# Index rows, key-bias rows and softmax sums taken from TensorE to VectorE, and the score weights requested first on SyncE's queue

## The chip, the cores and the metric

One NeuronCore of a Trainium2 chip runs the whole kernel. The metric is device microseconds of one execution. Five engines run their own instruction streams and meet at semaphores: TensorE (PE; its weight loads are shown apart as PEld), VectorE (DVE), ScalarE (ACT), GpSimd (POOL) and SyncE (SP), whose queue issues nearly all DMAs.

## The reference

Per batch of 8, ten rows of `base_hidden` (224 x 512) are chosen by a linear score, attend with 16 heads of 32 columns to 750 rows of `scaffold_hidden`, and the result replaces those ten rows.

```python
scores = jnp.einsum('bnd,d->bn', base_hidden, score_w[0]) + score_b[0]
_, topk_idx = jax.lax.top_k(scores, TOPK)                      # TOPK = 10
sparse_hidden = jnp.take_along_axis(base_hidden, topk_idx[:, :, None], axis=1)
q = (sparse_hidden @ Wq.T + bq).reshape(B, TOPK, H, dh).transpose(0, 2, 1, 3)
k = (scaffold_hidden @ Wk.T + bk) ...                          # same for v, with S = 750
logits = jnp.einsum('bhqd,bhkd->bhqk', q, k) * scale
attn = jax.nn.softmax(logits, axis=-1)
o = jnp.einsum('bhqk,bhkd->bhqd', attn, v).transpose(0, 2, 1, 3).reshape(B, TOPK, D)
attn_out = o @ out_w.T + out_b
return base_hidden.at[jnp.arange(B)[:, None], topk_idx].set(attn_out)
```

## The kernel before

Everything is float32. The key and value projections are folded away: `fold_keys` and `fold_pairs` multiply the queries by Wk, so that the logits of a batch are 24 matmuls of the raw context (`logits_by_step`, line 773, `logits`, line 787: six tiles of 125 context rows by four steps of 128 columns, for 160 query-head columns), and `weigh` (line 806) is 24 matmuls that weigh the raw context with the probabilities; `project_values` (821) and `project_output` (834) follow once, at the end. In the trace each of these float32 matmuls is two records, so a batch's `weigh` is 48.

Batches 0 and 1 go first (group 0). Their ten rows are found by ranking and taken from `x_sb` with one-hot matrices; the other six batches (group 1) go by VectorE's `choose_eight` and `choose_rest`, and GpSimd fetches their rows with an indirect DMA (line 286) that waits for `idx_ready`. The row numbers of all 80 rows stand in `row_idx`, one for each partition. Before the change they get there over TensorE: `move_idx` multiplies the one-hot matrices by `row_name` (677) and `idx_diag` by ones (678), and VectorE casts the PSUM column (456). That piece stands inside `weigh(0)`, ahead of its sixth matmul.

`dot_key_bias` (748) is query times key bias: 32 equal columns `key_rep` as weights, and the spread-out queries `q_diag` (each head's columns zero elsewhere; 40 columns for each batch) as the moving side. ScalarE (343, group 0) or VectorE (488, group 1) copies the result to `key_rows`, and a transposing reduction (493) makes `key_dot` of it.

The softmax's shift comes over VectorE: `find_max` (503) and `find_shift` (509 to 527) and `subtract_max` (535); ScalarE takes the exponential (352), which `weigh` of that batch waits for; `sum_probs` (541) adds over the six tiles. The sum over partitions is `sum_rows` (755), eight records on TensorE inside the last `weigh`, then a reciprocal over 128 x 320 (546). `finish_heads` (552, 555) needs it.

SyncE's queue issues in this order: x(0) to x(2), wq, x(3), wk, x(4), the first part of the context columns of batch 0, x(5), two more parts, x(6), a part of batch 1, x(7), two parts of batch 1, then the context rows `ctx_r` of batches 0 and 1 (200). `score(b)` (404) is VectorE's dot product of x(b) with the score weights, which TensorE spreads over the partitions (631) as soon as `score_line` is in; that 2 KB row was requested by ScalarE's queue (298).

Of the kernel before, what the change touches and what calls it, by code (L numbers as in the profile page):

```python
# [17 lines left out]
ALU = mybir.AluOpType  # L18
# [6 lines left out]
P = 128  # L25
# [28 lines left out]
def build(nc, x, x_lines, ctx_rows, ctx_cols, wq, wk, wv, wo, in_bias, out_b, score_row, out):  # L54
# [5 lines left out]
    with stack:  # L60
# [42 lines left out]
        idx_diag = sb("idx_diag", [GB, BQ])  # L103
# [8 lines left out]
        key_rep = sb("key_rep", [P, DT, QUAD])  # L112
        key_rows = sb("key_rows", [QUAD, B, DT, HC])
        key_dot = sb("key_dot", [QUAD, B, CB])
# [7 lines left out]
        prob_sum = sb("prob_sum", [S_P, B, HQ])  # L122
# [25 lines left out]
        row_idx_ps = misc_ps[1][0:BQ, N:N + 1]  # L148
# [17 lines left out]
        idx_diag_done, idx_moved, idx_ready = sem("idx_diag_done"), sem("idx_moved"), sem("idx_ready")  # L166
# [8 lines left out]
        key_rep_done, key_rows_done = sem("key_rep_done"), sem("key_rows_done")  # L175
        key_dot_ps, key_dot_done = sem("key_dot_ps"), sem("key_dot_done")
        heads_scaled = sem("heads_scaled")
        shifted, exp_done, sum_done, den_done = sem("shifted"), sem("exp_done"), sem("sum_done"), sem("den_done")
        inv_done = sem("inv_done")
# [11 lines left out]
        def _(sp):  # L191
# [16 lines left out]

            load_x(0, 3)
# [3 lines left out]
            load_x(4, 5)  # L213
            load_cols_part(0, 0)
            load_x(5, 6)
# [37 lines left out]
        def _(pool):  # L253
# [15 lines left out]
            pool.memset(idx_diag[:, :], 0.0).then_inc(consts_cleared, 1)  # L269
# [3 lines left out]
            pool.memset(idx_diag[0:1, TOPK:2 * TOPK], float(N)).then_inc(own_done, 1)  # L273
            pool.memset(regroup[:, :, :], 0.0).then_inc(regroup_done, 1)
            pool.memset(head_mask[:, :], 0.0).then_inc(mask_done, 1)
            for i in range(2 * FIRST):
# [8 lines left out]
            pool.wait_ge(idx_ready, 1)  # L285
# [11 lines left out]
        def _(act):  # L297
            act.dma_start(score_line[:, :], score_row).then_inc(score_w_in, 16)
# [41 lines left out]
            def copy_key_rows():  # L340
                act.wait_ge(key_dot_ps, 1)
                for e in range(DT):
                    nc.scalar.activation(
                        key_rows[:, 0:FIRST, e, :],
                        key_ps[0][e * QUAD:(e + 1) * QUAD, 0:HC * FIRST].rearrange("p (b c) -> p b c", b=FIRST),
                        ACT.Copy).then_inc(key_rows_done, 1)

# [18 lines left out]
            copy_key_rows()  # L366
# [25 lines left out]
        def _(dve):  # L392
# [36 lines left out]
            def choose_rest():  # L429
# [8 lines left out]
                    out=idx_diag[0:nb, b0 * TOPK:b1 * TOPK].rearrange("p (b q) -> p b q", q=TOPK),  # L438
# [44 lines left out]
            def copy_key_dot(g):  # L483
                b0, b1 = GROUPS[g]
                if g:
                    dve.wait_ge(key_dot_ps, 2)
                    for e in range(DT):
                        nc.vector.tensor_copy(
                            key_rows[:, b0:b1, e, :],
                            key_ps[g][e * QUAD:(e + 1) * QUAD, 0:HC * (b1 - b0)].rearrange("p (b c) -> p b c", b=b1 - b0))\  # L490
                            .then_inc(key_rows_done, 1)
# [4 lines left out]
                    AX.X, ALU.max, apply_transpose=True).then_inc(key_dot_done, 1)  # L496
# [42 lines left out]
            def sum_probs(b, n):  # L539
                dve.wait_ge(exp_done, 2 * b + 2)  # L540
                nc.vector.tensor_reduce(prob_sum[:, b, :], probs[n][:, :, :].rearrange("p t c -> p c t"), AX.X, ALU.add)\  # L541
                    .then_inc(sum_done, 1)

            def invert():
                dve.wait_ge(den_done, 1)
                nc.vector.reciprocal(inv_sum[:, :, :].rearrange("p e q -> p (e q)"), misc_ps[0][:, 0:DT * BQ]).then_inc(inv_done, 1)  # L546

            def finish_heads():
                dve.wait_ge(inv_done, 1)
# [8 lines left out]
            def finish_output():  # L558
# [29 lines left out]
            nc.vector.tensor_copy(key_rep[:, :, :], bias_sb[:, 1, :].unsqueeze(2).broadcast_to([P, DT, QUAD]))\  # L588
                .then_inc(key_rep_done, 1)
            dve.wait_ge(mask_done, 1 + HPT)  # L590
            spread_queries(0)
            score(4)
            score(5)
            copy_key_dot(0)
# [6 lines left out]
            choose_rest()  # L601
            find_max(1, 1)
            move_idx()
# [6 lines left out]
            copy_key_dot(1)  # L610
# [5 lines left out]
            invert()  # L616
# [5 lines left out]
        def _(pe):  # L622
# [50 lines left out]
            def move_idx():  # L673
                b0, b1 = GROUPS[1]
                pe.wait_ge(idx_diag_done, 1)
                for j in range(2):
                    nc.tensor.matmul(row_idx_ps, one_hot[:, j, :], row_name[:, j:j + 1], start=(j == 0), stop=False)
                nc.tensor.matmul(row_idx_ps, idx_diag[0:b1 - b0, :], ones[0:b1 - b0, 0:1], start=False, stop=True)\
# [237 lines left out]
```

## Time and profile before

| | us |
|---|---|
| runs of the kernel before | 143.16 median of 3 (143.11 to 146.93) |
| the profiled execution | 142.52, of which the span of the core is 140.7 |
| TensorE busy | 134.0 (95% of the span), 1312 matmul records |
| VectorE busy | 80.4 (57%) |
| ScalarE busy | 25.9 (18%) |
| GpSimd busy | 6.1 (4%) |
| DMA traffic | 37.52 MB, mean 267 GB/s over the span, 400 to 440 GB/s in nearly all of the first 31 us |
| granted TensorE clock | 1.00 of full speed in every stretch up to 120 us |

The chain of waits is the work that ended last, followed back: each piece was released by the one before it. A piece has its start and its length. A group's idle time before it says what it waited for.

### The profile page before, as it was taken

Reading aid. Unit: us, or ns where it says so; the run is one execution under the profiler, and the core shown is the slowest. Engines: PE = TensorE matmul, PEld = TensorE weight load, DVE = VectorE, ACT = ScalarE, POOL = GpSimd, SP = SyncE. Lnnn points to the kernel's source line nnn. Section 1 sums busy time; section 2 is a strip of 40 time slices with the busy share of each in tenths; the row PEclk is TensorE's granted clock in tenths of the full one; section 3 lists DMA queues with packets and bytes.
Section 4 is the critical chain, followed back from the end, with each engine's and each line's share of the span. In section 5 each row is a group of like instructions: output and inputs, shape, how many; then the busy total and the mean of one; then the engine's idle time right before and its main releaser. Section 6 shows DMA issues by size and latency. Waiting matters only on the chain.

```text
span 140.7 us, 3072 instructions
## 1 busy us (share of the span) xinstructions
PE 134.0 (95%) x1312; PEld 127.1 (90%) x1312; DVE 80.4 (57%) x212; ACT 25.9 (18%) x57; POOL 6.1 (4%) x31
## 2 busy tenths in 40 slices
PE   4989999999999999999999999999999999999990
PEld 2567999899999989999999999999999999998970
DVE  1788545999951576288870674088128605754350
ACT  4122410030411240003140041005001400411110
POOL 7400000003000000000000000000000000000002
PEclk9999999999999999999999999999999999999997
DMA  4999999999996299899979976995880380000001
GB/s 138 417 417 418 408 413 399 439 423 433 412 359 286 42 383 399 295 397 410 426 288 290 321 318 188 323 319 219 269 298 11 57 356 38 0 0 5 0 5 49
DMA packets 6959, 37.52 MB, mean 267 GB/s; under 512 B 961, under 2 KB 961, under 8 KB 4642
## 3 DMA queue, kind: packets, MB, share of 16 engines
q1 hardware_dynamic: 6528, 37.00, 69.3%
q0 software_dynamic: 128, 0.33, 0.7%
q8 instruction: 10, 0.16, 0.5%
q10 hardware_dynamic: 290, 0.01, 0.2%
q14 instruction: 3, 0.02, 0.0%
HBM read 33.50 MB, written 3.83 MB: 265 GB/s over the span
## 4 chain that ended last, share of the span: by engine, by line
PE 72%; DMA 14%; SPq 7%; issue 2%; DVE 1%; POOLq 1%; POOL 0%; DVEq 0%
PE mix_ps L806 38%; PE logits_ps L787 23%; DMA ctx_r<-ctx_rows_dram 14%; PE logits_ps L773 5%; SPq L197 3%; SPq L204 3%; PE logits_ps L737 2%; PE logits_ps L703 1%; PE mix_ps L737 1%; POOLq L60 1%; DVE o_T L555 1%; PE misc_ps L821 1%; DVE heads L552 1%; PE misc_ps L755 0%; SPq L210 0%
## 5 line engine op out<-in xcount | busy, mean ns | idle before, releaser
L806 PE MATMUL mix_ps<-probs,ctx_r 125*128 125x160 f32 x384 | 54.3, 301 | 0.1
L806 PEld LDWEIGHTS mix_ps<-probs,ctx_r 125*128 125x128 f32 x384 | 52.6, 190 | 0.9 <-issue 0.5
L787 PE MATMUL logits_ps<-qk,ctx_c 128*125 128x160 f32 x240 | 33.4, 299 | 0.0
L787 PEld LDWEIGHTS logits_ps<-qk,ctx_c 128*125 128x125 f32 x240 | 32.9, 188 | 0.0
L503 DVE TENSOR_REDUCE col_max<-logits_ps 125x160 f32<-125x960 f32 x8 | 9.2, 1154 | 25.5 <-PE logits_ps L787 21.2
L773 PE MATMUL logits_ps<-qk,ctx_c 128*125 128x160 f32 x144 | 20.5, 302 | 0.1
L773 PEld LDWEIGHTS logits_ps<-qk,ctx_c 128*125 128x125 f32 x144 | 19.6, 188 | 0.8 <-issue 0.4
L356 ACT ACTIVATE mix<-mix_ps 128x320 f32<-128x320 f32 x16 | 7.0, 439 | 64.4 <-PE mix_ps L806 64.4
L541 DVE TENSOR_REDUCE prob_sum<-probs 125x160 f32<-125x960 f32 x8 | 14.7, 1846 | 4.0 <-ACT probs L352 4.0
L352 ACT ACTIVATE probs<-probs 125x480 f32<-125x480 f32 x16 | 9.3, 603 | 27.9 <-DVE probs L535 27.9
L404 DVE CUSTOM_DVE_ANT_0 product<-x_sb,score_w_sb 112x513 f32<-112x513 f32 x16 | 10.4, 690 | 4.1 <-DMA x_sb<-x_lines_dram 4.1
L535 DVE TENSOR_TENSOR probs<-logits_ps,shift 125x480 f32<-125x480 f32 x16 | 9.8, 653 | 0.3
L625 PE MATMUL logits_ps<-ones 128*128 128x256 f32 (+2 forms) x8 | 4.1, 629 | 1.1 <-DVE ones L568 1.1
L290 POOL MEMSET pool_woken<- 16x1 f32 x1 | 0.1, 88 | 100.3 <-DVE o_T L555 100.3
L525 DVE COPY head_shift<-head_shift 32x5 f32<-32x5 f32 x24 | 3.9, 163 | 0.8
L513 DVE COPY quad_max<-quad_max 32x5 f32<-32x5 f32 x24 | 3.8, 158 | 0.8
L546 DVE RECIPROCAL inv_sum<-misc_ps 128x320 f32<-128x320 f32 x1 | 2.2, 2157 | 3.5 <-PE misc_ps L755 3.5
L703 PEld LDWEIGHTS logits_ps<-picked_T,wq_sb 128*64 128x64 f32 x128 | 3.9, 138 | 0.2 <-issue 0.2
L703 PE MATMUL logits_ps<-picked_T,wq_sb 128*64 128x20 f32 (+1 forms) x128 | 4.1, 218 | 0.0
L464 DVE TENSOR_TENSOR q_sb<-logits_ps,bias_sb 128x40 f32<-128x40 f32 (+1 forms) x4 | 1.0, 242 | 5.0 <-PE logits_ps L703 5.0
L637 PEld LDWEIGHTS mix_ps<-mix,ones 112*112 112x112 f32 x8 | 1.8, 284 | 1.5 <-ACT mix L306 1.5
L625 PEld LDWEIGHTS logits_ps<-ones 128*128 128x128 f32 x8 | 1.7, 258 | 1.4 <-DVE ones L568 1.1
(121 smaller groups left out, 88.7 us busy)
## 6 DMA issues: line engine op xcount, KB each, us to landing
ctx_r<-ctx_rows_dram SPq DMA_DIRECT2D x8, 1536.0 KB, 7.6
ctx_c<-ctx_cols_dram SPq DMA_DIRECT2D x6, 1500.0 KB, 10.1
x_sb<-x_lines_dram SPq DMA_DIRECT2D x8, 520.0 KB, 9.4
out_dram<-x_sb SPq DMA_DIRECT2D x8, 448.0 KB, 12.4
ctx_c<-ctx_cols_dram SPq DMA_DIRECT2D x2, 750.0 KB, 14.5
ctx_c<-ctx_cols_dram SPq DMA_DIRECT2D x4, 375.0 KB, 15.5
wq_sb<-wq_dram SPq DMA_DIRECT2D x1, 1024.0 KB, 7.4
wk_sb<-wk_dram SPq DMA_DIRECT2D x1, 1024.0 KB, 9.9
```

The lines of the kernel that those rows point to most:

```text
L197: sp.dma_start(ctx_c[b][:, fs, :, :], ctx_cols[b, :, fs, :, :]).then_inc(part_cols_in[b][k], 16)
L352: nc.scalar.activation(part, part, ACT.Exp, scale=SCALE).then_inc(exp_done, 1)
L356: nc.scalar.activation(mix[:, 2 * half:2 * half + 2, :, b * TOPK:(b + 1) * TOPK], mix_ps[half][:, 0:2 * HQ].rearrange("p (t h q) -> p t h ...
L404: nc.vector.tensor_tensor_reduce(out=products[j][:, :], in0=x_sb[0:X_P, b, j, 0:D + 1], in1=score_w_sb[:, :], scale=1.0, scalar=0.0, op0=A ...
L503: nc.vector.tensor_reduce(col_max[0:S_P, :], tiles(n).rearrange("p k t c -> p c k t"), AX.XY, ALU.max)\
L535: nc.vector.tensor_tensor(probs[n][:, k * BANK_T:(k + 1) * BANK_T, :], tiles(n)[:, k, :, :], shift[0:S_P, :].unsqueeze(1).broadcast_to([S_ ...
L541: nc.vector.tensor_reduce(prob_sum[:, b, :], probs[n][:, :, :].rearrange("p t c -> p c t"), AX.X, ALU.add)\
L625: nc.tensor.matmul(logits_ps[1][:, 1, 0:n], ones[:, :], ones[:, 0:1].broadcast_to([P, n]), start=True, stop=True)
L703: last = nc.tensor.matmul(query_ps[g][half][j * TILE:(j + 1) * TILE, k * nq:(k + 1) * nq], wq_sb[:, t, c:c + TILE], picked_T[g][:, t, b0 * ...
L773: last = nc.tensor.matmul(logits_ps[n][0:S_P, t // BANK_T, (t % BANK_T) * HQ:(t % BANK_T + 1) * HQ], ctx_c[n][:, f, t, :], qk[:, b, f, :], ...
L787: last = nc.tensor.matmul(logits_ps[n][0:S_P, t // BANK_T, (t % BANK_T) * HQ:(t % BANK_T + 1) * HQ], ctx_c[n][:, f, t, :], qk[:, b, f, :], ...
L806: last = nc.tensor.matmul(mix_ps[half][:, f * HQ:(f + 1) * HQ], ctx_r[n][0:S_P, t, c:c + P], probs[n][:, t, :], start=(t == 0), stop=(t == ...
```

## The change

Five things change. (1) SyncE's queue issues the score row before everything else, instead of ScalarE's. (2) The first part of batch 0's context columns is issued ahead of x(4) and x(5). (3) `move_idx` leaves TensorE: VectorE adds the rows of `idx_diag` in a transposing reduction (three columns of 32), and four new steps (`name_first`) make the first 20 row numbers, between the key-bias rows and `score(5)`. `move_idx` now stands ahead of `find_max(1)`. (4) `dot_key_bias` takes the narrow queries `q_sb` as the moving side and the bias split by head, `key_heads`, as weights; VectorE multiplies the result with slices of `ident` to spread it over the heads (`spread_key_dot`), for both groups, ScalarE no longer copies. (5) `sum_rows` and the large reciprocal are replaced by `invert`, all on VectorE, once for batches 0 to 6 after `sum_probs(6)` and once for batch 7 after `sum_probs(7)`. TensorE no longer waits for `inv_done`; `finish_heads` does.

```diff
+            sp.dma_start(score_line[:, :], score_row).then_inc(score_w_in, 16)
             load_x(0, 3)
             sp.dma_start(wq_sb[:, :, :], wq).then_inc(wq_in, 16)
             load_x(3, 4)
             sp.dma_start(wk_sb[:, :, :], wk).then_inc(wk_in, 16)
-            load_x(4, 5)
             load_cols_part(0, 0)
-            load_x(5, 6)
+            load_x(4, 6)
...
+            def name_first():
+                dve.wait_ge(names_cleared, 1)
+                cols = slice(0, FIRST * TOPK)
+                nc.vector.tensor_scalar(named[0][0:X_P, cols], one_hot[:, 0, cols], row_name[:, 0:1], None, ALU.mult)\
+                    .then_inc(name_step, 1)
...
+                nc.vector.scalar_tensor_tensor(out=named[1][0:X_P, cols], in0=one_hot[:, 1, cols], scalar=row_name[:, 1:2],
+                                               in1=named[0][0:X_P, cols], op0=ALU.mult, op1=ALU.add).then_inc(name_step, 1)
...
+                nc.vector.tensor_reduce(quad_named[:, 0:1], named[1][:, :].unsqueeze(1), AX.X, ALU.add, apply_transpose=True)\
+                    .then_inc(name_step, 1)
...
             def move_idx():
-                dve.wait_ge(idx_moved, 1)
-                nc.vector.tensor_copy(row_idx[:, :], row_idx_ps).then_inc(idx_ready, 1)
+                dve.wait_ge(idx_diag_done, 1)
+                nc.vector.tensor_reduce(idx_cols[:, :], idx_diag[:, :, :], AX.X, ALU.add, apply_transpose=True).then_inc(idx_summed, 1)
+                dve.wait_ge(idx_summed, 1)
+                dve.wait_ge(name_step, 7)
+                nc.vector.tensor_tensor(row_idx[0:QUAD, :], idx_cols[:, 0:1], first_idx[:, :], ALU.add).then_inc(idx_ready, 1)
+                for k in range(1, QUADS - 1):
+                    m = min(QUAD, BQ - k * QUAD)
+                    nc.vector.tensor_copy(row_idx[k * QUAD:k * QUAD + m, :], idx_cols[0:m, k:k + 1]).then_inc(idx_ready, 1)
...
+            def spread_key_dot(g):
...
+                    nc.vector.tensor_tensor(
+                        key_rows[:, b0:b1, e, :].rearrange("p b (h q) -> p b h q", h=HPT),
+                        key_ps[g][lines, 0:nb * TOPK].rearrange("p (b q) -> p b q", b=nb).unsqueeze(2).broadcast_to([QUAD, nb, HPT, TOPK]),
+                        ident[lines, e * QUAD:e * QUAD + HPT].unsqueeze(1).unsqueeze(3).broadcast_to([QUAD, nb, HPT, TOPK]), ALU.mult)\
+                        .then_inc(key_rows_done, 1)
...
+            def invert(part, b0, b1):
+                at = 7 * part
+                bs = slice(b0, b1)
+                dve.wait_ge(key_dot_done, 2)
+                dve.wait_ge(sum_done, b1)
+                nc.vector.tensor_reduce(
+                    quad_sum[:, 0, bs, :].rearrange("p b k -> p (b k)"),
+                    prob_sum[:, bs, :].rearrange("p b c -> p (b c)").rearrange("p (k c) -> p k c", c=QUAD),
+                    AX.X, ALU.add, apply_transpose=True).then_inc(inv_step, 1)
...
+                for q in range(1, QUADS):
+                    nc.vector.tensor_copy(quad_sum[0:QUAD, q, bs, :], quad_sum[q * QUAD:(q + 1) * QUAD, 0, bs, :])\
+                        .then_inc(inv_step, 1)
...
+                nc.vector.tensor_reduce(all_sum[:, bs, :], quad_sum[0:QUAD, :, bs, :].rearrange("p q b k -> p b k q"), AX.X, ALU.add)\
+                    .then_inc(inv_step, 1)
...
+                nc.vector.reciprocal(inv_all[:, bs, :], all_sum[:, bs, :]).then_inc(inv_step, 1)
...
+                nc.vector.transpose(inv_rows[:, bs, :].rearrange("p b c -> p (b c)").rearrange("p (k c) -> p k c", c=QUAD),
+                                    inv_all[:, bs, :].rearrange("p b k -> p (b k)").unsqueeze(2)
+                                    .broadcast_to([QUAD, (b1 - b0) * CB, QUAD])).then_inc(inv_step, 1)
...
+                for h in range(HPT):
+                    nc.vector.tensor_copy(
+                        inv_sum[h * DH:(h + 1) * DH, :, :].rearrange("p e (b q) -> p e b q", b=B)[:, :, bs, :],
+                        inv_rows[:, bs, :].rearrange("p b (e h q) -> p h e b q", e=DT, h=HPT)[:, h]).then_inc(inv_done, 1)
...
-            weigh(0, 0, {5: move_idx})
+            weigh(0, 0, {})
...
-            weigh(B - 1, (B - 1) % 2, {14: sum_rows})
+            weigh(B - 1, (B - 1) % 2, {})
```

GpSimd clears four more tiles at the start (`key_heads`, `named`, a part of `prob_sum`, and a larger `idx_diag`).

On TensorE's queue, from the end of `logits` of batch 1 into `weigh(0)` and `weigh(1)`, there stands before:

```order
L773 MATMUL logits_ps<-qk,ctx_c 125x160 x16
L806 MATMUL mix_ps<-probs,ctx_r 128x160 x5
L677 MATMUL misc_ps<-row_name,one_hot 80x1 x2
L678 MATMUL misc_ps<-ones,idx_diag 80x1
L806 MATMUL mix_ps<-probs,ctx_r 128x160 x33
L685 MATMUL logits_ps<-ident,picked 128x80 x4
```

and of the changed kernel:

```order
L812 MATMUL logits_ps<-qk,ctx_c 125x160 x16
L845 MATMUL mix_ps<-probs,ctx_r 128x160 x38
L734 MATMUL logits_ps<-ident,picked 128x80 x4
```

The three matmuls inside `weigh(0)` are gone, and nothing stands between `logits` of batch 1 and the transposes of the fetched rows but 38 matmuls of `weigh`.

On VectorE's queue, from the index arithmetic of `choose_rest` to the first step of `find_shift(1)`, there stands before:

```order
L437 SCALAR_TENSOR_TENSOR idx_diag<-top_idx,row_base,own_batch 6x60
L503 TENSOR_REDUCE col_max<-logits_ps 125x160
L456 CAST row_idx<-misc_ps 80x1
L509 TENSOR_REDUCE quad_max<-col_max 128x5
L513 COPY quad_max<-quad_max 32x5 x3
```

and of the changed kernel:

```order
L440 SCALAR_TENSOR_TENSOR idx_diag<-top_idx,row_base,own_batch 6x60
L476 TENSOR_REDUCE idx_cols<-idx_diag 32x3
L479 TENSOR_TENSOR row_idx<-idx_cols,first_idx 32x1
L482 CAST row_idx<-idx_cols 32x1
L482 CAST row_idx<-idx_cols 16x1
L532 TENSOR_REDUCE col_max<-logits_ps 125x160
L538 TENSOR_REDUCE quad_max<-col_max 128x5
```

Four small instructions have come ahead of `find_max(1)`, and the one cast behind it is gone.

On the same queue, from the end of `score(4)` to `find_max(0)` (the rows named ISA are `score`), there stands in the changed kernel:

```order
L516 TENSOR_TENSOR key_rows<-logits_ps,ident 32x2x40 x4
L522 TENSOR_REDUCE key_dot<-key_rows 32x10
L460 TENSOR_SCALAR named<-one_hot,row_name 112x20
L463 SCALAR_TENSOR_TENSOR named<-one_hot,row_name,named 112x20
L466 TENSOR_REDUCE quad_named<-named 128x1
L470 COPY quad_named<-quad_named 32x1 x3
L472 TENSOR_REDUCE first_idx<-quad_named 32x1
L407 ISA product,scores<-x_sb,score_w_sb 112x513
L407 ISA scores 112x1
```

Before, `score(5)` followed `score(4)` at once, and of these rows there was only the reduction to `key_dot`, behind `score(5)`; eleven instructions more now stand ahead of `score(5)`.

## Rows read from the trace of the kernel before

**Rows 1.** The page: shares of the chain of waits by engine.

```profile
PE 72%; DMA 14%; SPq 7%; issue 2%; DVE 1%; POOLq 1%; POOL 0%; DVEq 0%
```

**Rows 2.** Waits: engine and line, what for, us in total, times, longest.

```profile
PEld mix_ps L806 <- DMA ctx_r<-ctx_rows_dram: 0.3, 1, 0.3
```

**Rows 3.** The chain of waits in order of time: start, length, what.

```profile
0.82 0.38 SPq L204
...
11.56 19.48 DMA ctx_r<-ctx_rows_dram
...
31.08 1.63 PE mix_ps L806 x10
32.70 0.22 PE misc_ps L677 x4
...
33.15 9.16 PE mix_ps L806 x66
...
51.55 0.54 PE misc_ps L748 x8
...
58.80 6.52 PE logits_ps L787 x48
```

**Rows 4.** Timeline, 32 to 38 us: start, length, engine, line, what.

```profile
32.04 0.27 DVE L437 SCALAR_TENSOR_TENSOR idx_diag<-top_idx,row_base,own_batch 6x60 f32<-6x60 uint32 x1
32.24 1.14 DVE L503 TENSOR_REDUCE col_max<-logits_ps 125x160 f32<-125x960 f32 x1
...
33.31 0.14 DVE L456 CAST row_idx<-misc_ps 80x1 uint32<-80x1 f32 x1
...
33.73 1.08 POOL L286 DMA_INDIRECT picked<-x_dram,row_idx  x1 [27.95 <-DVE row_idx L456]
33.79 0.54 DVE L513 COPY quad_max<-quad_max 32x5 f32<-32x5 f32 x3
...
36.68 1.17 ACT L352 ACTIVATE probs<-probs 125x480 f32<-125x480 f32 x2 [0.95 <-DVE probs L535]
```

**Rows 5.** The tile picked: from the issue of its DMA to landing.

```profile
DMA to landing us min/median/max: 7.8/7.8/7.8
```

**Rows 6.** Timeline of VectorE, 18 to 24 us.

```profile
18.93 0.70 DVE L404 CUSTOM_DVE_ANT_0 product<-x_sb,score_w_sb 112x513 f32<-112x513 f32 x1 [2.58 <-DMA x_sb<-x_lines_dram]
...
22.13 0.69 DVE L404 CUSTOM_DVE_ANT_0 product<-x_sb,score_w_sb 112x513 f32<-112x513 f32 x1 [1.47 <-DMA x_sb<-x_lines_dram]
...
23.88 1.16 DVE L503 TENSOR_REDUCE col_max<-logits_ps 125x160 f32<-125x960 f32 x1 [0.43 <-PE logits_ps L773]
```

**Rows 7.** First part of the context columns: its issue, and its time to landing.

```profile
L197 SPq DMA_DIRECT2D ctx_c<-ctx_cols_dram x1: 448/448/448, 4.4 to 4.4; - x1
...
DMA to landing us min/median/max: 12.0/12.0/12.0
```

**Rows 8.** Timeline of SyncE's queue: the issue behind its waits for x(0) to x(7).

```profile
24.51 0.33 SPq L193 DMA_DIRECT2D ctx_c<-ctx_cols_dram  x1
```

**Rows 9.** VectorE operations by line: ns min/median/max, or the group's mean.

```profile
L493 DVE TRANSPOSE_TENSOR_REDUCE key_dot<-key_rows x2: 494/830/1167, 20.2 to 53.9; 32x10 f32<-32x320 f32 x1, 32x30 f32<-32x960 f32 x1
...
L488 DVE COPY key_rows<-misc_ps x4: 393/400/409, 52.2 to 53.4; 32x240 f32<-32x240 f32 x4
...
L546 DVE RECIPROCAL inv_sum<-misc_ps 128x320 f32<-128x320 f32 x1 | 2.2, 2157 | 3.5 <-PE misc_ps L755 3.5
```

**Rows 10.** Timeline of VectorE, 110 to 118 us: find_max(7) and the idle ahead.

```profile
117.54 1.16 DVE L503 TENSOR_REDUCE col_max<-logits_ps 125x160 f32<-125x960 f32 x1 [5.53 <-PE logits_ps L787]
```

**Rows 11.** The chain of waits, 117 to 134 us.

```profile
117.50 10.32 PE mix_ps L806 x76
127.82 0.68 PE misc_ps L755 x8
128.50 2.92 PE mix_ps L806 x20
...
133.07 0.25 DVE heads L552
```

More of the change, by code:

```diff
@@ L102, in build @@
         top_idx = sb("top_idx", [GB, 16], U32)
-        idx_diag = sb("idx_diag", [GB, BQ])
+        idx_diag = sb("idx_diag", [QUAD, QUADS - 1, QUAD])
+        idx_cols = sb("idx_cols", [QUAD, QUADS - 1])
+        named = [sb(f"named{j}", [P, QUAD]) for j in range(2)]
+        quad_named = sb("quad_named", [P, QUADS])
+        first_idx = sb("first_idx", [QUAD, 1])
         row_idx = sb("row_idx", [BQ, 1], U32)
@@ L587, in _ @@
             dve.wait_ge(bias_in, 16)
-            nc.vector.tensor_copy(key_rep[:, :, :], bias_sb[:, 1, :].unsqueeze(2).broadcast_to([P, DT, QUAD]))\
-                .then_inc(key_rep_done, 1)
             dve.wait_ge(mask_done, 1 + HPT)
+            dve.wait_ge(heads_cleared, 1)
+            nc.vector.tensor_tensor(key_heads[:, :, 0:HPT], bias_sb[:, 1, :].unsqueeze(2).broadcast_to([P, DT, HPT]),
+                                    head_mask[:, :].unsqueeze(1).broadcast_to([P, DT, HPT]), ALU.mult).then_inc(key_heads_done, 1)
             spread_queries(0)
             score(4)
+            spread_key_dot(0)
+            name_first()
             score(5)
-            copy_key_dot(0)
             score(6)
@@ L601, in _ @@
             choose_rest()
+            move_idx()
             find_max(1, 1)
-            move_idx()
             find_shift(1)
@@ L609, in _ @@
             copy_pairs()
-            copy_key_dot(1)
+            spread_key_dot(1)
             for b in range(2, B):
@@ L615, in _ @@
                 sum_probs(b, b % 2)
-            invert()
+                if b >= B - 2:
+                    invert(b - B + 2, 0 if b == B - 2 else B - 1, b + 1)
             finish_heads()
@@ L671, in join_rows @@
                     last.then_inc(picked_T_ps[0], 1)
[L673 to L678, printed above, removed]
-                    .then_inc(idx_moved, 1)
             def transpose_picked():
@@ L743, in dot_key_bias @@
             def dot_key_bias(g):
-                w = HC * (GROUPS[g][1] - GROUPS[g][0])
-                pe.wait_ge(key_rep_done, 1)
-                pe.wait_ge(q_done, 2 * g + 2)
+                w = TOPK * (GROUPS[g][1] - GROUPS[g][0])
+                pe.wait_ge(key_heads_done, 1)
+                pe.wait_ge(q_biased, 2 * g + 2)
                 for e in range(DT):
-                    last = nc.tensor.matmul(key_ps[g][e * QUAD:(e + 1) * QUAD, 0:w], key_rep[:, e, :],
-                                            q_diag[g][:, e, :, :, :].rearrange("p b h q -> p (b h q)"), start=True, stop=True)
+                    last = nc.tensor.matmul(key_ps[g][e * QUAD:(e + 1) * QUAD, 0:w], key_heads[:, e, :],
+                                            q_sb[g][:, e, :, :].rearrange("p b q -> p (b q)"), start=True, stop=True)
                 last.then_inc(key_dot_ps, 1)
-            def sum_rows():
-                pe.wait_ge(sum_done, B)
-                for h in range(HPT):
-                    last = nc.tensor.matmul(misc_ps[0][h * DH:(h + 1) * DH, 0:DT * BQ], ones[0:S_P, 0:DH],
-                                            prob_sum[:, :, :].rearrange("p b (e h q) -> p h e b q", e=DT, h=HPT)[:, h],
-                                            start=True, stop=True)
-                last.then_inc(den_done, 1)
             def logits_by_step(b, n, copied, between):
```

79 lines of the change are left out of this document (41 added, 38 removed).

## The prediction

> **What bounds the kernel now.** I read the chain of waits first, then the waits of the single engines, then the timelines around the edited places. The chain is TensorE for 72%, with DMA (14%) and SyncE's issuing (7%) ahead of it [rows 1]. In order of time it has two parts. Up to 31.04 us it is SyncE's queue and the stream of loads that ends with the context rows of batch 0 (issued at 11.56, 19.48 us to landing). From 31.08 us on TensorE runs nearly without a gap: 48 records of `logits` or `weigh` take 6.52 us, 0.136 us each [rows 3], up to the value projection and VectorE's first `heads` at 133.07 [rows 11]. So there are two prices: a record taken off TensorE after 31 us is worth its time, unless something else is late there; before 31 us only what moves the stream counts, because TensorE has 0.3 us of slack against `ctx_r`, for which it waited so long [rows 2].
>
> **The change, part by part.**
>
> *Score row first on SyncE.* An issue on that queue takes 0.38 us at the start, and the first x is issued at 0.82 [rows 3]. All loads behind the score row go out one issue later: 0.4 us. The stream is never without work afterwards, so `ctx_r(0)` lands 0.4 us later, at 31.45, and `weigh(0)` starts there: +0.4. Bounds: 0, if the stream makes the slot good, and 0.8, two slots. What the row gives is an earlier score chain; but `logits(0)` needs the next parts of the context columns, which are as late as the rest, and `ctx_r(0)` still ends the stage, so I cost that gain at 0. In sentences of their own, on the notes: the Trainium skill ("DMA: Bandwidth & Descriptors", Issuing engines are not separate DMA queues) says that all issuing engines feed the same 16 DMA engines, and that a second issuer only saves the sequencer's time of initiating. By that rule the move to SyncE brings the score row no sooner and costs SyncE one slot, the same +0.4 that the issue row gives; by the reading that a small row gets in ahead of the heavy ones, the early chain would gain some tenths that end at the same wait. No row here tells the two apart.
>
> *Context columns ahead of x(4), x(5).* The first part landed at 4.38 + 12.0 = 16.4 [rows 7]. In the changed order x(4) is complete only where that part was, at 16.4 + 0.4 = 16.8; x(5), which VectorE had at 18.93, comes at 19.3, and x(6), had at 22.13, at 22.5 [rows 6]. `score(4)` thus ends at 18.1 (a score is two records of 0.69, started 0.6 apart, so 1.3).
>
> *VectorE between score(4) and find_max(0).* `spread_key_dot(0)`: four multiplies of 32 x 80 from PSUM. The trace has none of that form; the nearest are a copy of 32 x 240 from PSUM at 0.40 and the tiny cast at 0.14 [rows 4, 9]. I take 0.25, between them, 1.0 in all (bounds 0.6 and 1.6), and 0.5 for the reduction of 32 x 320 [rows 9]. `name_first`: seven small instructions; three dependent-free copies take 0.54, so 0.18 each, and with the transposing reduction of 128 x 32 I take 1.4 (bounds 1.0 and 2.0). VectorE is through at 18.1 + 1.5 + 1.4 = 21.0, or with waits 21.1; `score(5)` to 22.4, `score(6)` from 22.5 to 23.8, `find_max(0)` at 23.85 against 23.88 before [rows 6]. So this is hidden with 0.1 us to spare, and that is thin: what overruns goes into everything that follows on VectorE. x(7) had landed by 24.51 [rows 8], 24.9 with the delay; `score(7)` began at 25.0: no wait. (The Trainium skill, "VectorE: DVE Perf Modes", The TRN2 errata, gives (N + 151)/0.96 ns for a float32 `tensor_tensor`, an estimate of 0.24 us at N = 80; by it the four multiplies would be 0.96. No row here has that size.)
>
> *move_idx.* TensorE loses the piece from 32.70 to 33.15: 0.45. The 66 records behind it took 9.16 where 66 x 0.136 is 8.96: a restart of 0.20 goes too. Together 0.65 [rows 3]. Before, TensorE came to `weigh(1)` at 33.15 + 0.20 + 38 x 0.136 = 38.5. Now it starts at 31.45, has the first 10 records at 1.63 (0.27 over their share) and ends 48 at 31.45 + 6.52 + 0.27 = 38.24: a gain of 0.26, the 0.65 less the 0.4. But `weigh(1)` also needs the exponential of batch 1, and `find_max(1)` now stands behind four instructions. They are, from the start of `idx_diag` at 32.04: 0.31 for it with its wait, 0.26 for a reduction of 32 x 96 (by the two sizes of line 493, 1.05 ns an element above 0.16), 0.04 for its wait, 0.14 and 2 x 0.18. That makes 33.15, against 32.24: +0.91 [rows 4, 9]. The first exponential of batch 1 ended at 36.68 + 0.60 = 37.28; now 38.19, and with the signal 38.23. TensorE arrives at 38.24. The two tie, so any further lateness of VectorE is paid in full there, and any further earliness of TensorE is lost there. I take **-0.26**, bounds -0.26 and +0.5. Behind VectorE's chain stand `subtract_max(1)`, two `sum_probs` and the queries of group 1, with some microseconds of idle time on VectorE ahead of the last. The fetch of the rows starts sooner: `row_idx` was whole at 33.45 and is now at 33.1; GpSimd issued 0.28 later and the rows took 7.8 us [rows 4, 5], so 41.2 instead of 41.5, and TensorE wants them at 42.0: no wait.
>
> *dot_key_bias.* For group 1 it took 0.54 for 240 moving columns [rows 3], now 60. Group 0's, at 80 columns, is off the end of the chain. I take half, 0.28, for 60 columns, as the weight loads remain: **-0.26** (bounds 0 and -0.35). VectorE's four copies of 0.40 become four multiplies of about 0.41, and VectorE then idles until `logits` of batch 2 is done.
>
> *sum_rows.* TensorE loses 127.82 to 128.50, 0.68, and a restart: 20 records took 2.92 against 2.72. **-0.88** (bounds -0.68 and -0.95) [rows 11].
>
> *invert.* Part 0 on VectorE after `sum_probs(6)`: transposing reduction of 1120 elements 1.33 (line 493's slope), three copies 0.6, reduction of 140 elements 0.3, reciprocal of 35 elements 0.3 (320 took 2.16, 6.7 ns each), transpose of 1120 elements 1.35 by the same slope, four strided copies of 280 elements 0.45 each, and seven signals 0.3: about 6.0 [rows 9]. The cover is 5.53 us of idle time ahead of `find_max(7)` [rows 10] and behind that 1.4 us: from `find_max` to the first exponential batch 1 took 37.28 - 32.24 = 5.04 [rows 4], so batch 7's was ready at 117.54 + 5.04 = 122.6, and `weigh(7)` began at 117.50 + 6.52 = 124.0 (the 76 records there are all of `weigh(6)` and 28 of `weigh(7)`) [rows 11]. So 6.9 us are hidden, and above that each microsecond is paid. Part 1, with 160 elements, costs about 2.7. It follows the second exponential (123.2) and a `sum_probs` of under 2 us, so it ends before 128; `heads` wants it at 133.07 - 1.40 = 131.7 [rows 11]: hidden. Nothing: **0**.
>
> Sum: -0.26 - 0.26 - 0.88 = -1.40. The profiled execution took 142.52 (span 140.7 and 1.8 around it), so 141.1; its time is 0.64 below the median of the runs, 143.16. Against that median, which a new median will be compared with, -1.40 gives **141.8**.
>
> **The rivals.** *VectorE overruns ahead of find_max(0).* The multiplies from PSUM or the naming steps cost up to 1.0 more than I have. For it: the spare is 0.1. Against: every price lies between rows. An overrun of 0.5 to 1.0 moves the exponential of batch 1 by as much and leaves 0.9 to 0.4 of the gain: 142.3 to 142.8. The same comes of x(4) landing late.
>
> *The load stream is later than one slot*, by 0.5 to 1.0: `weigh(0)` starts at 32.0 to 32.4 and 0.5 to 1.0 of the gain goes: 142.3 to 142.8. For it: the stream's tail ends the first stage. Against: the bytes are the same.
>
> *invert(0) is too long, and the kernel is slower.* The place is `find_max(7)`, and it decides from 6.9 us. For it: the transpose reads a broadcast input and the copies stride over heads, forms without a row. Against: the slopes. If its two large operations and four copies cost double, it is 10.5 us, 3.6 above the cover, and the sum is +2.2: 145.4. Below 8.3 us it is not slower than before. The Trainium skill ("VectorE: DVE Perf Modes", Why `tensor_reduce` can't reduce along partition axis) says that VectorE cannot reduce over partitions. Line 493 does so within blocks of 32 here, in 0.49 us, and three copies join the blocks, so the trace decides against it; the rule would change only whether such steps are possible.
>
> *It does not do what it says.* TensorE's records at the two places were no real load, and the restart costs stay: then only 0.45 + 0.68 of records go, of which 0.4 is paid to the stream, with nothing for `dot_key_bias`: -0.7, 142.5.
>
> *More than forecast.* The 0.4 is not paid and VectorE is 0.4 earlier than I have it: -1.8, 141.4; with the executions as low as the profiled one, 140.8.
>
> **How the numbers follow.** Forecast (-1.1 to -1.6) 0.5; VectorE's overrun 0.17; a later stream 0.1; only the records 0.08; more than forecast 0.1; slower through `invert` 0.05. The likeliest gives 141.8. The range takes in the first five cases, and the profiled execution's lower level at the low end: 140.8 to 143.1. The line for faster or slower is 2% (2.86 us), about what a measurement of this kernel can tell from no change. No gain case reaches it but with a low run: 0.04 faster; the long `invert` gives nearly all of 0.04 slower; 0.92 within.
>
> **What would show it.** In the changed profile: the first issue of x at 1.2 instead of 0.82; `weigh(0)` starting near 31.45 behind `ctx_r`; `find_max(0)` near 23.9 and `find_max(1)` near 33.15; `weigh(1)` starting near 38.25 with TensorE and the exponential within 0.1 of each other; `dot_key_bias` of group 1 near 0.28; an unbroken 48 records in `weigh(7)` and `heads` waiting for TensorE, not for `inv_sum`; `find_max(7)` at most 0.5 behind the last matmul of `logits`. It is wrong where TensorE waits at `weigh(1)`, at the transposes of the fetched rows or at `weigh(7)` for longer than 0.2 us.

## The result, and the profile after

| | before | after |
|---|---|---|
| median of the runs | 143.05 us (9 runs) | 141.80 us (9 runs) |
| profiled execution | 142.52 us, span 140.7 | 141.41 us, span 139.6 |
| ratio of times, 95% | | 0.991 (0.990 to 0.993), or -1.25 us |

The forecast was 141.8. Some executions of every kernel here, the kernel before among them, take 2 to 4 us longer from their first microseconds on; the medians in this table contain them, the ratios and all later medians leave them out, and of the traces of e1, e3, e4 and after_again, which are of such executions, only lengths are read, and when the score row was first used.

The page of after: the chain's shares by engine, which answer to [rows 1].

```profile
PE 72%; DMA 13%; SPq 8%; issue 3%; DVE 1%; POOLq 1%; POOL 0%; DVEq 0%
```

After, the chain of waits in order of time (start, length, what), answering to [rows 3, 11]:

```profile
0.82 0.33 SPq L217
...
13.11 18.27 DMA ctx_r<-ctx_rows_dram
31.43 6.79 PE mix_ps L845 x48
38.21 0.11 issue
38.32 4.04 PE mix_ps L845 x28
42.37 0.28 PE logits_ps L734 x4
...
51.60 0.24 PE misc_ps L795 x8
51.84 6.71 PE logits_ps L812 x48
...
117.25 13.04 PE mix_ps L845 x96
130.29 0.41 PE misc_ps L858 x16
...
131.95 0.25 DVE heads L606
```

I read it from the end. `weigh(6)` and `weigh(7)` are 96 unbroken records of 13.04 us, where [rows 11] have 76 + 8 + 20 in 13.92: `sum_rows` and its restart, 0.88, are gone. `dot_key_bias(1)` is 0.24 instead of 0.54. But the first transpose of the fetched rows (L734) starts at 42.37; before, the same record started at 42.31 (1.63 + 0.22 + 0.23 + 9.16 from 31.08). So the whole stage ahead of it gained nothing: between `weigh(0)` and `weigh(1)` there is now a gap of 0.11, and the 28 records behind it take 4.04 where 28 x 0.136 is 3.81, a restart of 0.23.

After, waits (engine and line, what for, us in total, times, longest), answering to [rows 2]:

```profile
PEld mix_ps L845 <- DMA ctx_r<-ctx_rows_dram: 0.4, 1, 0.4
...
PEld mix_ps L845 <- issue: 0.3, 1, 0.3
```

After, timeline of VectorE, ScalarE and TensorE around the moved steps, answering to [rows 4, 6]:

```profile
2.34 0.87 PEld L688 LDWEIGHTS mix_ps<-score_line,ones 1*112 1x112 f32 x4 [0.70 <-DMA score_line<-score_row_dram]
...
16.82 0.70 DVE L407 CUSTOM_DVE_ANT_0 product<-x_sb,score_w_sb 112x513 f32<-112x513 f32 x1 [2.39 <-DMA x_sb<-x_lines_dram]
...
18.05 1.03 DVE L516 TENSOR_TENSOR key_rows<-logits_ps,ident 32x80 f32<-32x80 f32 x4
...
22.51 0.70 DVE L407 CUSTOM_DVE_ANT_0 product<-x_sb,score_w_sb 112x513 f32<-112x513 f32 x1 [0.27 <-DMA x_sb<-x_lines_dram]
...
23.85 1.16 DVE L532 TENSOR_REDUCE col_max<-logits_ps 125x160 f32<-125x960 f32 x1
...
33.16 1.16 DVE L532 TENSOR_REDUCE col_max<-logits_ps 125x160 f32<-125x960 f32 x1
...
37.62 1.17 ACT L356 ACTIVATE probs<-probs 125x480 f32<-125x480 f32 x2 [2.19 <-DVE probs L564]
```

x(4) at 16.82, four multiplies in 1.03, x(6) at 22.51 after a wait of 0.27, `find_max(0)` at 23.85 behind `score(6)` and with no wait for TensorE, `find_max(1)` at 33.16, the exponential of batch 1 from 37.62. TensorE's `weigh(1)` starts 0.70 after the exponential does.

After, timeline, `invert(0)` on VectorE, answering to [rows 10]:

```profile
111.92 1.34 DVE L579 TRANSPOSE_TENSOR_REDUCE quad_sum<-prob_sum 128x35 f32<-128x1120 f32 x1
113.29 0.58 DVE L585 COPY quad_sum<-quad_sum 32x35 f32<-32x35 f32 x3
113.91 0.39 DVE L588 TENSOR_REDUCE all_sum<-quad_sum 32x35 f32<-32x140 f32 x1
114.33 0.36 DVE L591 RECIPROCAL inv_all<-all_sum 32x35 f32<-32x35 f32 x1
114.72 1.33 DVE L593 STREAM_TRANSPOSE key_rows<-inv_all 32x1120 f32<-32x1120 f32 x1
116.09 1.28 DVE L598 COPY inv_sum<-key_rows 32x280 f32<-32x280 f32 x4
117.40 1.16 DVE L532 TENSOR_REDUCE col_max<-logits_ps 125x160 f32<-125x960 f32 x1
```

From 111.92 to 117.40 it is 5.5 us, and the 5.53 us of idle time of [rows 10] is filled. `find_max(7)` follows the last record of `logits` (117.25) by 0.15, and `weigh(7)` doesn't feel it.

### The profile page after: what moved, and what is told of

It reads as the page before. It is cut to its first block, busy times and chain, and to the rows that moved or that the text cites. A ratio compares the mean times of both kernels' runs of the same rounds, so it can differ in the third digit from the quotient of the medians.

```text
span 139.6 us, 3090 instructions
## 1 busy us (share of the span) xinstructions
PE 132.7 (95%) x1298; PEld 126.4 (91%) x1298; DVE 88.4 (63%) x247; ACT 24.9 (18%) x53; POOL 7.8 (6%) x34
## 4 chain that ended last, share of the span: by engine, by line
PE 72%; DMA 13%; SPq 8%; issue 3%; DVE 1%; POOLq 1%; POOL 0%; DVEq 0%
PE mix_ps L845 38%; PE logits_ps L826 23%; DMA ctx_r<-ctx_rows_dram 13%; PE logits_ps L812 5%; SPq L205 4%; SPq L212 3%; PE logits_ps L784 2%; PE logits_ps L750 1%; PE mix_ps L784 1%; POOLq L60 1%; DVE o_T L609 1%; PE misc_ps L858 1%; DVE heads L606 1%; PE logits_ps L858 0%; SPq L221 0%
## 5 line engine op out<-in xcount | busy, mean ns | idle before, releaser
L606 DVE TENSOR_TENSOR heads<-misc_ps,inv_sum 128x80 f32<-128x80 f32 x2 | 0.5, 238 | 4.3 <-PE misc_ps L858 4.3
```

## The experiments

The theory: the gain is that of the two matmul groups that left TensorE (`sum_rows` 0.88, `dot_key_bias` 0.30); the index part gives nothing, because `weigh(1)` then waits for VectorE. Rivals: the 0.65 of `move_idx` is a gain that something else took back (the score row's slot on SyncE), or VectorE is late through x(4).

### One part alone

**e1_sums_only**: the kernel before, with `sum_rows` taken off TensorE.

```
-            weigh(B - 1, (B - 1) % 2, {14: sum_rows})
+            weigh(B - 1, (B - 1) % 2, {})
-            invert()
+                if b >= B - 2:
+                    invert(b - B + 2, 0 if b == B - 2 else B - 1, b + 1)
```

> The kernel before with the softmax sums alone moved to VectorE. My theory is that this part is most of the gain: the piece of 0.68 us and the restart behind it go, 0.87 us in all, so the time is 0.87 us below before (ratio 0.994), find_max(7) starts at most 0.1 us behind the last matmul of logits, and invert is hidden. The rival is that taking records off TensorE at one place lets something else end later (the copy of mix or the heads' wait for inv_sum), and the gain is under 0.5 us.

Measured: 0.993 (0.991 to 0.995), or -1.0 us (-0.7 to -1.3). Its chain of waits has the same unbroken piece:

```profile
120.85 13.04 PE mix_ps L834 x96
133.90 0.41 PE misc_ps L847 x16
```

Most of the change's gain is here, and `invert` costs nothing that is seen.

**e2_dot_only**: the kernel before, with the narrow product for the key bias.

```
-                    last = nc.tensor.matmul(key_ps[g][e * QUAD:(e + 1) * QUAD, 0:w], key_rep[:, e, :],
-                                            q_diag[g][:, e, :, :, :].rearrange("p b h q -> p (b h q)"), start=True, stop=True)
+                    last = nc.tensor.matmul(key_ps[g][e * QUAD:(e + 1) * QUAD, 0:w], key_heads[:, e, :],
+                                            q_sb[g][:, e, :, :].rearrange("p b q -> p (b q)"), start=True, stop=True)
```

> The kernel before with the narrow key-bias product alone. My theory: group 1's piece goes from 0.54 to 0.24 us and nothing else moves, so 0.30 us below before (ratio 0.998). The rival: the four multiplies of group 0 on VectorE delay score(6) or find_max(0) by some tenths, and with it the exponential of batch 1, and the gain is 0 or a loss of 0.2 us.

Measured: 0.996 (0.994 to 0.998), or -0.6 us (-0.3 to -0.8). Its chain:

```profile
31.75 1.36 PE mix_ps L811 x10
...
42.92 0.28 PE logits_ps L690 x4
...
52.16 0.24 PE misc_ps L753 x8
```

The piece at 52.16 is 0.30 shorter, as in after. The median says a little more than the trace, inside its interval. Note the 42.92: in this execution the early stage was 0.6 later than in the profiled one of before, with the score row on ScalarE's queue and nothing changed about the indices. The four multiplies aren't the reason: TensorE waited 1.73 us for the first part of the context columns and began `logits` of batch 0 at 17.78 (17.05 in before). One trace of an early stage doesn't settle tenths there.

**e3_index_only**: the kernel before, with the row indices summed on VectorE.

```
-            weigh(0, 0, {5: move_idx})
+            weigh(0, 0, {})
-            find_max(1, 1)
             move_idx()
+            find_max(1, 1)
```

> The kernel before with the row indices alone moved to VectorE; the request order of the loads is that of before. My theory: weigh(0) starts at 31.08 us as before and ends at 37.87 instead of 38.5, but find_max(1) starts 0.93 us later, the exponential of batch 1 is ready at 38.2, TensorE waits 0.35 us and restarts for 0.24, and the time is that of before within 0.1 us. The rival is that the records taken off count in full and it was the later stream of loads that took them back in the changed kernel: then it is 0.65 us faster than before (ratio 0.9955).

Measured: 1.001 (0.999 to 1.003): nothing. The rival, the full 0.65 as a gain of its own (0.995), falls, and the score row's slot isn't what took it, since this kernel has the row where before had it. Its chain shows what did:

```profile
41.17 0.79 issue
```

TensorE, done with `weigh(0)`, stands still ahead of `weigh(1)`. I take the kind of the wait from it, not its size; after has the same gap with 0.11.

The three parts add up to -1.0 - 0.6 + 0.1 = -1.5, the whole change measured -1.25. What is left, +0.25, is the score row and the order of the loads together; the intervals are wide enough to hold it or nothing.

### The score row back on ScalarE

**e4_row_on_act** and, once more, **e4b_row_on_act** (the same code), with **after_again** (the changed kernel again) beside it on one chip.

```
-            sp.dma_start(score_line[:, :], score_row).then_inc(score_w_in, 16)
             load_x(0, 3)
...
+            act.dma_start(score_line[:, :], score_row).then_inc(score_w_in, 16)
             act.dma_start(bias_sb[:, :, :], in_bias).then_inc(bias_in, 16)
```

> The changed kernel with the request for the score row back on ScalarE's queue. My theory: the loads come 0.4 us earlier and weigh(0) starts at 31.05 instead of 31.43, but weigh(1) still begins with the exponential of batch 1 at 38.3, so the time is that of the changed kernel within 0.1 us; the row lands near 3.1 us instead of 2.3, and the first logits start 0.7 us later, which costs nothing. The rival: the slot on SyncE is paid in the time, and this kernel is 0.4 us faster than the changed one. A second rival: the early chain counts, and this one is up to 0.7 us slower.

> The changed kernel with the score row requested by ScalarE, once more, beside the changed kernel on one chip. Theory 1 (VectorE's chain to the exponential of batch 1 binds at weigh(1), not the load stream): equal to the changed kernel within 0.1 us. Theory 2 (the slot on SyncE is paid): 0.3 to 0.4 us faster, with every x and every part of the context columns landing 0.4 us earlier and find_max(0) starting earlier.

> The changed kernel once more, so that the next three stand beside it on the same chip. My theory of its middle: weigh(0) starts behind ctx_r or behind logits of batch 1, and weigh(1) waits 0.1 to 0.8 us for the exponential of batch 1. The ratio should again be 0.9913 within 0.002.

Measured: e4 0.988 (0.985 to 0.990), e4b 0.990 (0.986 to 0.993), after_again 0.994 (0.991 to 0.996). Both times the version with the row on ScalarE is ahead, by 0.5 us (e4 against the first runs of after) and 0.6 (e4b against after_again, same chip), though in each pair the intervals overlap; e8 and e9 below are the clearer pair. My expectation, that the slot on SyncE is hidden by the exponential of batch 1, doesn't hold. after_again's times lie in two groups, 141.67 to 141.89 and 142.51 to 142.83.

The timeline and chain of e4b:

```profile
2.28 0.87 PEld L688 LDWEIGHTS mix_ps<-score_line,ones 1*112 1x112 f32 x4 [0.65 <-DMA score_line<-score_row_dram]
...
17.84 0.69 DVE L407 CUSTOM_DVE_ANT_0 product<-x_sb,score_w_sb 112x513 f32<-112x513 f32 x1 [3.47 <-DMA x_sb<-x_lines_dram]
...
24.52 1.16 DVE L532 TENSOR_REDUCE col_max<-logits_ps 125x160 f32<-125x960 f32 x1
...
26.95 0.09 PEld L701 LDWEIGHTS misc_ps<-ident,scores 112*6 112x6 f32 x2 [0.79 <-DVE scores L407]
...
38.19 0.79 issue
38.98 4.04 PE mix_ps L845 x28
```

Two things. The row from ScalarE's queue is there at 2.28, no later than the 2.34 from SyncE's in after. And this is the rival "VectorE overruns, x(4) is late" in full: x(4) comes 1.0 later than in after, `find_max(0)` 0.67 later, TensorE waits 0.79 for the scores in the middle of `logits(1)` and 0.79 for the exponential. This execution took 141.97, the longest of the five that its ratio rests on.

### Around find_max(1)

**e5_max_first**: after, with `find_max(1)` ahead of `move_idx`. **e6_late_pick**: the same, and the transposes of the fetched rows three matmuls (six records) later, the query projection one.

```
-            move_idx()
             find_max(1, 1)
+            move_idx()
...   only e6:
-            weigh(1, 1, {14: transpose_picked, 19: lambda: project_queries(1)})
+            weigh(1, 1, {17: transpose_picked, 20: lambda: project_queries(1)})
```

> The changed kernel with find_max(1) ahead of the index steps on VectorE. My theory: the exponential of batch 1 comes 0.9 us earlier and weigh(1) starts with the end of weigh(0), without the wait of 0.1 and the restart of 0.24; but the row indices come 1.16 us later, the fetch lands at 42.4, and TensorE waits 0.3 us for it at 42.05 and restarts. Time as the changed kernel within 0.15 us. The rival, that the fetch has slack: 0.3 us faster.

> As the kernel with find_max(1) first, and TensorE's transposes of the fetched rows three matmuls later in weigh(1), the query projection one later. My theory: neither the exponential nor the fetch is waited for, and the index part gives back what the prediction had for it: 0.3 to 0.4 us faster than the changed kernel (ratio to before about 0.989). The rival, that the shorter distance from the projection to fold_pairs makes TensorE wait for q_diag: no gain.

Measured: e5 142.12 and 142.31, two executions, too few for a ratio; e6 0.992 (0.989 to 0.996), the same as after. The chain of e5:

```profile
25.00 1.16 DVE col_max L532
...
32.15 6.52 PE mix_ps L845 x48
38.67 0.55 issue
39.23 4.04 PE mix_ps L845 x28
```

A miss: from `find_max(0)` to the exponential of batch 1 (38.52) it is 13.52 here, 13.77 in after. I had expected the whole cost of `move_idx` to leave that path, but `find_shift(1)` needs the maxima and comes behind `move_idx` in either order, so only 0.25 went. e6's trace says the same (13.52, and TensorE waits 0.55 at `weigh(1)`, where I had expected no wait). For the fetched rows TensorE waited in neither, so the 0.3 that I had expected for it in e5 isn't there.

### The idle time ahead of x(4)

VectorE waits 2.4 to 3.8 us for x(4), and the twelve instructions of `spread_key_dot(0)` and `name_first` don't need it. So: **e7_no_index** (after without the index part), **e8_steps_early** (after, with the steps ahead of `score(4)`), **e9_early_row_on_act** (e8 with the row on ScalarE), **e10_no_index_early** (e9 without the index part).

```
e8, e9:
+            name_first()
+            spread_key_dot(0)
             score(4)
-            spread_key_dot(0)
-            name_first()
e7, e10:
-            weigh(0, 0, {})
+            weigh(0, 0, {5: move_idx})
```

> The changed kernel with the index part undone (row indices over TensorE again, no name_first). Theory V, formed from the runs so far: the index part gives nothing, since the 0.65 us that TensorE loses is matched by VectorE's longer chain to the exponential of batch 1, at which weigh(1) then waits. So this kernel is at the changed one within 0.2 us, TensorE starts weigh(1) without a wait, and find_max(0) starts before 24.0 even where x(4) lands at 18. Rival P: TensorE's records count in full, and this kernel is 0.65 us slower than the changed one.

> The changed kernel with name_first and spread_key_dot(0) ahead of score(4) on VectorE, that is in the idle time ahead of x(4). Theory V: in the executions in which x(4) lands near 18 us, VectorE's chain from it to find_max(0) is what ends last (find_max(0) at 24.5 to 25.0 and a wait of 0.5 to 0.8 us at weigh(1)); with 3.0 us of steps moved into the idle time, find_max(0) starts by 23.9 in all of them, the wait falls to 0.1 to 0.4 and the fast runs lie at 141.3 to 141.8, a ratio near 0.990. Rival: the load stream sets find_max(0) and weigh(1) anyway, and nothing changes.

> As the kernel with the two steps early, and the score row requested by ScalarE. Theory V: the stream is 0.4 us earlier, but weigh(1) begins with the exponential of batch 1, whose chain starts behind logits(0); this one waits for parts of the context columns, so 0.1 to 0.3 us of the 0.4 come through. Rival (the slot costs nothing at all): equal to the kernel with the two steps early.

> The changed kernel without the index part, with spread_key_dot(0) ahead of score(4) and the score row requested by ScalarE: only the parts that paid. Theory V: weigh(0) at 31.1, the index piece of 0.65 inside it, no wait at weigh(1): 1.2 us below before, 141.8, a ratio near 0.992. Rival: VectorE's shorter chain lets weigh(1) start earlier than in any other kernel here and the ratio is 0.988.

| | score row | executions | their median (range) | ratio to before (95%) |
|---|---|---|---|---|
| e7 | SyncE | 5 | 142.11 (141.54 to 142.22) | 0.993 (0.990 to 0.997) |
| e8 | SyncE | 10 | 141.73 (141.30 to 143.02) | 0.992 (0.989 to 0.995) |
| e9 | ScalarE | 4 | 141.06 (140.96 to 141.19) | 0.987 (0.984 to 0.991) |
| e10 | ScalarE | 4 | 141.47 (141.32 to 141.59) | 0.990 (0.987 to 0.994) |

The four were measured side by side on one chip, so their times can be compared directly; the intervals of their ratios overlap.

- *The row off SyncE* (e9 against e8, which differ in nothing else): 0.7 us. All four executions of e9 are below all ten of e8. That is more than the 0.1 to 0.3 that I expected, and more than the 0.33 that the issue takes; why, no run here shows.
- *The index part* (e9 against e10): 0.4 us, again without overlap, four executions against four (I had expected 0.992 for e10). e7 against after gives 0.3 by the ratios, where I had expected at most 0.2, and against after_again (0.994) nothing.
- *The steps ahead of `score(4)`* (e8 against after and after_again, 0.991 and 0.994): no gain shown. My expectation, `find_max(0)` by 23.9, was missed in the trace:

```profile
22.76 0.69 DVE L407 CUSTOM_DVE_ANT_0 product<-x_sb,score_w_sb 112x513 f32<-112x513 f32 x1 [1.22 <-DMA x_sb<-x_lines_dram]
...
24.17 1.16 DVE L532 TENSOR_REDUCE col_max<-logits_ps 125x160 f32<-125x960 f32 x1
...
38.25 0.38 issue
```

VectorE is done early and then waits 1.22 for x(6), so the load stream sets `find_max(0)`: the rival that I had written down for e8. It does so in after too, where x(6) was read at 22.51 after a wait of 0.27.

e9 is the fastest kernel of the study, about 1.8 us below before and 0.6 below after. Its timeline and chain:

```profile
3.10 0.87 PEld L688 LDWEIGHTS mix_ps<-score_line,ones 1*112 1x112 f32 x4 [1.47 <-DMA score_line<-score_row_dram]
...
17.02 1.03 DVE L516 TENSOR_TENSOR key_rows<-logits_ps,ident 32x80 f32<-32x80 f32 x4 [0.61 <-PE logits_ps L795]
...
22.31 0.69 DVE L407 CUSTOM_DVE_ANT_0 product<-x_sb,score_w_sb 112x513 f32<-112x513 f32 x1 [1.29 <-DMA x_sb<-x_lines_dram]
...
23.66 1.16 DVE L532 TENSOR_REDUCE col_max<-logits_ps 125x160 f32<-125x960 f32 x1
...
31.18 6.79 PE mix_ps L845 x48
37.96 0.14 issue
38.10 4.04 PE mix_ps L845 x28
```

The steps ran before `score(4)`, and VectorE has 1.29 us of slack in front of x(6) that after did not have (0.27 there). The score row landed at 3.10, the latest but one of all traces, in an execution of the fastest kernel (141.19): a row 0.8 later doesn't show in its time.

The early stage of the traces (starts in us; the last column is the transposes of the fetched rows, L734 in after; in e6 they stand six records later):

| | `find_max(0)` | `weigh(0)` | exponential of batch 1 | gap ahead of `weigh(1)` | transposes |
|---|---|---|---|---|---|
| before | 23.88 | 31.08 | 36.68 | none, `move_idx` on TensorE | 42.31 |
| after | 23.85 | 31.43 | 37.62 | 0.11 | 42.37 |
| e2 | 24.60 | 31.75 | 37.41 | none, `move_idx` on TensorE | 42.92 |
| e4b | 24.52 | 31.67 | 38.28 | 0.79 | 43.02 |
| e5 | 25.00 | 32.15 | 38.52 | 0.55 | 43.27 |
| e6 | 24.91 | 32.06 | 38.43 | 0.55 | 43.99 |
| e7 | 24.03 | 31.89 | 37.37 | none, `move_idx` on TensorE | 43.13 |
| e8 | 24.17 | 31.46 | 37.92 | 0.38 | 42.67 |
| e9 | 23.66 | 31.18 | 37.40 | 0.14 | 42.15 |
| e10 | 23.58 | 31.10 | 36.57 | none, `move_idx` on TensorE | 42.34 |

Three readings.

*The index part.* With `move_idx` on TensorE, from `weigh(0)` to the transposes it is 11.23 or 11.24 in before, e7 and e10, and 11.17 in e2. With it on VectorE, ahead of `find_max(1)`, it is 10.94, 11.35, 11.21 and 10.97 (after, e4b, e8, e9). There the start of `weigh(1)` follows VectorE alone: the exponential comes 13.74 to 13.77 behind `find_max(0)`, and `weigh(1)` 0.70 or 0.71 behind that, in all four. TensorE would be ready 6.79 after `weigh(0)` (6.52 in e4b, where it came to `weigh(0)` without a pause), so the gap opens as soon as `find_max(0)` is later than `weigh(0)` less 7.7 (less 7.9 in e4b). The most that the index part gives in these traces is 0.3, and it costs 0.1 to 0.2 where VectorE is late.

*Behind the transposes.* The way to `heads` is 89.58 or 89.59 in the traces of after, e4b, e5 and e7 to e10 (131.95 - 42.37 in after), and was 90.76 before: -1.18, the same each time.

*The slot on SyncE.* Where `ctx_r` ended the stage, `weigh(0)` starts at 31.43, 31.46 and 31.89 with the row on SyncE (after, e8, e7), and at 31.18 and 31.10 with it on ScalarE (e9, e10). For e10, as an example of a kernel with the row off SyncE, the chain's pieces are:

```profile
12.79 18.26 DMA ctx_r<-ctx_rows_dram
31.10 1.62 PE mix_ps L829 x10
```

`ctx_r` landed at 31.05 there and at 31.38 in after. Its own issue isn't what decides (before issued it at 11.56, 1.2 earlier than e10, and it landed at 31.04); the whole stream is later. The slot is paid at `weigh(0)`, by 0.3 in e8 against e9, and it shows at x(6) as well, which VectorE read at 22.51, 22.64 and 22.76 with the row on SyncE (after, e7, e8) and at 22.31 and 22.23 with it on ScalarE (e9, e10). So VectorE and TensorE move together. That is what my expectation of e4 missed. x(4) shows no such order: 16.82 in after, 17.84 in e4b.

## Why the prediction was right, and where it was not

The range held, and so did the account of what bounds the kernel. That the time is right to the tenth is in part luck: the sum against the profiled execution was -1.40 and measured -1.11 (142.52 to 141.41), and it fell on 141.8 because the medians differed by 1.25 and that of before lay 0.11 lower than the one that I started from. The wait at `weigh(1)`, 0.11, stayed under the 0.2 that I had named as a sign of being wrong; other traces have 0.38 (e8) and 0.79 (e4b) there.

- *Score row*: +0.4 on the stream, `weigh(0)` at 31.45. Measured 31.43. The row gained nothing: its first reader started at 2.28 in ten traces, six with it on ScalarE's queue (e1 to e4, e4b, e10) and four with it on SyncE's (after_again, e5, e6, e7), and at 2.34 in after. The 3.17 of before's own trace, where that row stood 0.83 later than in after, comes back in e9 (3.10) from the same queue, so I take it for a spread of landings, not the queue's price. So the rule of the Trainium skill ("DMA: Bandwidth & Descriptors", Issuing engines are not separate DMA queues) holds here in both its parts: no earlier landing, and a slot paid. The price in time was larger than my 0.4: 0.5 to 0.7 in three pairs (e4, e4b, e9).
- *x(4) and VectorE up to find_max(0)*: 16.8 and 23.85 forecast, 16.82 and 23.85 measured; the multiplies 1.03 (1.0), `key_dot` 0.50 (0.5), `name_first` 1.38 (1.4). For x(4) that agreement is luck: in the other traces with this order of loads in which VectorE waited for it, it came at 17.84 to 18.32 (e4b, e5, e6, e7). With `name_first` behind it, `find_max(0)` then starts at 24.5 to 25.0 (e4b, e5, e6). The rival with 0.17 thus names what happens in some executions; I had given x(4) a sentence there and taken one arrival for fixed.
- *move_idx*: the term of the sum that failed. The records saved (0.65) and the tie at `weigh(1)` were right (TensorE 38.21, forecast 38.24; exponential 37.62, forecast 37.59). Wrong was to price a tie at 0. TensorE stood for 0.11, and the 28 records behind the gap take 0.23 over their share, as before the records behind the matmuls of `move_idx` took 0.20 over theirs. So one restart was replaced by another: -0.26 forecast, +0.06 measured. e3 shows the same as a time, 1.001 (0.999 to 1.003). The term can pay where the rest stands otherwise: 0.4 in e9 against e10.
- *dot_key_bias*: -0.26 forecast; 0.54 to 0.24, -0.30.
- *sum_rows*: -0.88 forecast, -0.88 measured, and e1 shows it as a time.
- *invert*: 6.0 forecast, 5.5 measured, part 1 2.5 for 2.7 (125.08 to 127.60). The large transposes were sized right (1.34 and 1.33), the strided copies of 280 elements too dear (0.30 each, not 0.45). Zero on the path, as forecast, and the rival of a slower kernel falls.
- *The fetch*: TensorE's transposes of the rows follow their predecessor without a wait; before and after the rows took 7.8.

What stays open: the two groups of times. They are there in the kernel before (beside e7 to e10: 142.44 to 142.92 and 143.19 to 143.30, and one at 144.23) and in e3 as well (142.25 to 142.62 and 143.29 to 143.47). A late x(4), which costs e4b 0.65 at the transposes, is of the right size for the distance between the groups of after_again, but no trace of after in its upper group was taken. e8, which takes VectorE's steps out of x(4)'s way, has nine runs between 141.30 and 142.07 and one at 143.02: in favour, no more. Nor was the order of x(4) and the context columns undone alone, so what part (2) of the change gives or costs isn't known.

## What to carry to other kernels

Where moving work between engines ends in a tie, price the tie: the engine that comes first pays the wait and its restart, and what it saved is lost (e3, nothing for 0.65 us of records). Keep small loads off the queue whose loads bound the start: one slot of 0.33 us there cost 0.5 to 0.7 us here, on both sides of the tie, and taking it off gave about half as much again as the change itself (e4, e9). Before moving steps into idle time ahead of one landing, look for the next landing behind it: in e8 VectorE then waited for x(6), and no gain was seen.

## What the runs showed of the hardware

- The first reader of a 2 KB load started at 2.28 in ten traces, from ScalarE's queue and from SyncE's alike, at 2.34 (after) and 2.43 (e8) from SyncE's, and at 3.10 (e9) and 3.17 (before) from ScalarE's. The issue began at 0.8 in all that were read for it (before, after, after_again, e4, e4b, e7 to e10).
- x(4), a load in the middle of the stream, came at 16.82 to 18.32 in five traces with the same order of the large loads (after, e4b, e5, e6, e7). In after the mean busy share of the 16 DMA engines was 1.00 to 1.04, that is full, in every stretch of 4 us from 4 to 24 us, and the end of the stream (`ctx_r`) moved by only 0.8 between traces (31.04 in before, 31.85 in e7).
- A transposing reduction and a transpose of 1120 elements cost the same on VectorE, 1.34 and 1.33 us; the transpose read a broadcast input, and no trace here has one that doesn't. The eleven instructions of `invert(0)` and the eleven of part 1 replace a matmul group of 0.68 and a reciprocal of 2.16 us ([rows 9, 11]) by 5.5 and 2.5 us that nobody waits for.
- A gap of only 0.11 us ahead of 28 records costs as much restart (0.23) as one of 0.79 does: the 28 records take 4.04 in after, e4b, e5, e8 and e9, with gaps of 0.11, 0.79, 0.55, 0.38 and 0.14.
